# Swapping a unit's similarities with a gather, and loading the first image by channel chunk

## The reference

```python
xn  = x / max(norm(x, axis=1), EPS)              # x: (8, 512, 32, 48), float32
cn  = centroids / max(norm(centroids, axis=1), EPS)       # 40 centroids of 512
sim = einsum('bchw,nc->bnhw', xn, cn)
idx = argmax(sim, axis=1);  onehot = one_hot(idx, 40)
sum_x = einsum('bhwn,bchw->bnc', onehot, x)      # sums of each image's clusters
mean  = sum_x / max(count, 1)
delta = mean[idx] - x                            # the gathered mean, less x
alpha = exp(-mean_over_channels(delta * delta))
y   = x + alpha * delta
out = relu(einsum('oc,bchw->bohw', W, y) + b)    # W: 512 x 512
```

## Time and profile before

| | |
|---|---|
| median of 3 runs | 421.4 us (420.66 to 421.58) |
| the profiled execution | 421.0 us |
| its span | 419.2 us |
| TensorE, matmuls | 410.0 us, 98% of the span |
| VectorE | 335.4 us, 80% |
| ScalarE | 256.0 us, 61% |
| GpSimd | 257.6 us, 61% |
| moved by DMA | 73.94 MB |

### The profile page before, as it was taken

One profiled execution on the slowest core, in us unless ns is written; L12 is line 12 of the kernel. 1 busy time (PEld: TensorE's weight loads), 2 busy tenths in 40 slices (PEclk: granted clock), 3 DMA queues, 4 the chain that ended last, 5 costly groups with the idle time before them and its releaser, 6 DMA issues.

```text
span 419.2 us, 5853 instructions
## 1 busy us (share of the span) xinstructions
PE 410.0 (98%) x2127; PEld 292.1 (70%) x2150; DVE 335.4 (80%) x411; ACT 256.0 (61%) x351; POOL 257.6 (61%) x113
## 2 busy tenths in 40 slices
PE   7999999999999999999999999999999999999996
PEld 6744466775767767775868757777777758777885
DVE  2469979689789889899798898898798997788730
ACT  5665374665764765665855666746756658566641
POOL 2000654993599766993879936996769938334420
PEclk9999999999999999999999999999999999999999
DMA  8999295987389384966669573893857220222223
GB/s 275 309 277 159 55 255 155 297 243 179 123 212 291 102 211 147 275 172 179 223 154 253 195 198 104 237 265 121 220 136 228 100 102 1 102 100 100 96 77 128
DMA packets 70927, 73.94 MB, mean 176 GB/s; under 512 B 2724, under 2 KB 45732, under 8 KB 70900
## 3 DMA queue, kind: packets, MB, share of 16 engines
q1 hardware_dynamic: 70900, 73.58, 63.2%
HBM read 48.40 MB, written 25.17 MB: 175 GB/s over the span
## 4 chain that ended last, share of the span: by engine, by line
PE 90%; DVE 3%; ACT 3%; issue 1%; DMA 1%; SPq 0%; DVEq 0%; ACTq 0%
PE main L886 20%; PE main L887 19%; PE main L888 19%; PE sump L828 9%; PE fa L779 9%; PE gat L861 5%; DMA x<-x 1%; PE fa L788 1%; PE al L868 1%; PE fa L803 1%; DVE xt L350 1%; PE main L929 1%; PE al L874 1%; PE gat L874 1%; PE main L901 1%
## 5 line engine op out<-in xcount | busy, mean ns | idle before, releaser
L886 PE MATMUL main<-yh,wh 128*128 128x512 f32 x376 | 152.8, 406 | 0.7 <-ACT o L602 0.7
L887 PE MATMUL main<-yl,wh 128*128 128x512 f32 x376 | 146.7, 390 | 0.0
L888 PE MATMUL main<-yh,wl 128*128 128x512 f32 x376 | 146.7, 390 | 0.0
L310 POOL TENSOR_TENSOR z<-z,x 128x1024 f32<-128x1024 f32 x42 | 99.8, 2396 | 68.3 <-DVE z L437 68.3
L317 POOL TENSOR_TENSOR yl<-z,yh 128x1024 fp32r<-128x1024 f32 x44 | 105.6, 2420 | 54.9 <-ACT yh L594 54.9
L602 ACT ACTIVATE o<-main,bcol 128x512 f32<-128x512 f32 x96 | 65.3, 682 | 61.8 <-PE main L888 61.7
L886 PEld LDWEIGHTS main<-yh,wh 128*128 128x128 f32 x376 | 70.6, 188 | 21.9 <-issue 5.0
L888 PEld LDWEIGHTS main<-yh,wl 128*128 128x128 f32 x376 | 70.6, 188 | 15.2
L887 PEld LDWEIGHTS main<-yl,wh 128*128 128x128 f32 x376 | 70.7, 188 | 13.8
L324 POOL TENSOR_TENSOR xr<-xt 128x2048 f32<-128x2048 f32 x11 | 51.5, 4681 | 20.8 <-DVE xt L350 20.8
L413 DVE TENSOR_TENSOR z<-gat,x 128x1024 f32<-128x1024 f32 x46 | 56.1, 1219 | 9.3 <-PE gat L861 9.0
(11 more groups left out here) (118 smaller groups left out, 378.7 us busy)
## 6 DMA issues: line engine op xcount, KB each, us to landing
x<-x SPq DMA_DIRECT2D x24, 1024.0 KB, 5.4
out<-o SPq DMA_DIRECT2D x23, 1024.0 KB, 7.2
xs<-x SPq DMA_DIRECT2D x84, 256.0 KB, 5.6
o<-w SPq DMA_DIRECT2D x1, 1024.0 KB, 12.3
out<-o SPq DMA_DIRECT2D x4, 256.0 KB, 2.1
sq<-centroids SPq DMA_DIRECT2D x2, 80.0 KB
bcol<-bias SPq DMA_DIRECT2D x1, 2.0 KB, 11.9
```

The costliest lines, as they stand in the source:

```text
L310: pool.tensor_tensor(z, z, X[g // PARTS % 2][:, pair(h), span(g)], ALU.add).then_inc(y_pool, 1)
L886: t_.matmul(main[:, o % 2, :], WH[:, k, rows], YH[g % 2][:, k, :], start=(k == 0), stop=False)
L887: t_.matmul(main[:, o % 2, :], WH[:, k, rows], YL[g % 2][:, k, :], start=False, stop=False)
L888: last = t_.matmul(main[:, o % 2, :], WL[:, k, rows], YH[g % 2][:, k, :], start=False, stop=(k == KC - 1))
```

## The change

Three things are edited.

1. In an image's second slot the similarities of the next image's third unit stand ahead of the second gather on TensorE, not behind it. ScalarE's copy of them stands ahead of the second square, and VectorE's first half transpose of unit g + 4 ahead of the second difference. There are six such slots, units 4, 7, 10, 13, 16 and 19.
2. Image 0's x is loaded by unit and channel chunk, in twelve DMAs of 256 KB, each with its own semaphore, and the similarities wait for each chunk just before they use it. The counts of the other x semaphores follow. Two of six warming matmuls go.
3. In the first slot of unit 3 alone, the relu of call 1 stands on ScalarE ahead of the second high half, not behind it.

```diff
@@ -153,6 +153,8 @@
             return gat[:, 0, :] if g == 1 else al[:, :]
 
 
+
+        first_in = [[sem(f"first_in{u}_{k}") for k in range(KC)] for u in range(PARTS)]
         x_in = [[sem(f"x_in{j}_{u}") for u in range(PARTS)] for j in range(2)]
         xs_in = [sem(f"xs_in{j}") for j in range(2)]
         w_in, b_in = sem("w_in"), sem("b_in")
@@ -230,6 +232,10 @@
                 if b >= 2:
                     for h in range(2):
                         wait_y(sp, g - 2 * PARTS, h)
+                if b == 0:
+                    for k in range(KC):
+                        sp.dma_start(X[0][:, k, span(g)], x_rows[0, :, k, span(g)]).then_inc(first_in[u][k], 16)
+                    return
                 sp.dma_start(X[b % 2][:, :, span(g)], x_rows[b, :, :, span(g)]).then_inc(x_in[b % 2][u], 16)
 
             def load_xs(g):
@@ -523,9 +529,11 @@
                     transpose_half(g + 3, 1)
                 scale(g - 1, 0)
                 scale(g - 1, 1)
+                if beside and p == 1:
+                    transpose_half(g + 4, 0)
                 delta(g, 1)
                 y_half(g - 1, 1)
-                if beside and p < 2:
+                if beside and p == 0:
                     transpose_half(g + 4, 0)
                 if beside and p == 2:
                     low_clusters(b + 1)
@@ -723,9 +731,11 @@
                     relu(g - 2, 0)
                     if g == PARTS:
                         exp(g - 1)
+                    if beside and p == 1:
+                        copy_sims(3 * b + 5)
                     square(g, 1)
-                    if beside:
-                        copy_sims(3 * b + 3 + 2 * p)
+                    if beside and p == 0:
+                        copy_sims(3 * b + 3)
                     high_half(g - 1, 0)
                     if beside and p == 0:
                         copy_sims(3 * b + 4)
@@ -734,8 +744,10 @@
                     move_upper(g)
                     if not beside:
                         high_sum(g)
+                    if g == PARTS:
+                        relu(g - 2, 1)
                     high_half(g - 1, 1)
-                    if beside and p == 0:
+                    if beside and p == 0 and g > PARTS:
                         relu(g - 2, 1)
                     if beside:
                         high_sum(g)
@@ -762,7 +774,8 @@
 
             def similarities(g):
                 b, u = divmod(g, PARTS)
-                pe.wait_ge(x_in[b % 2][u], 16 * (b // 2 + 1))
+                if b > 0:
+                    pe.wait_ge(x_in[b % 2][u], 16 * ((b + 1) // 2))
                 if b == 1:
                     pe.wait_ge(ohT_done, 1)
                 wait(pe, g_ready, b if b > 1 else 0)
@@ -770,6 +783,8 @@
                     pe.wait_ge(simS_done, PARTS * b + 1)
                 rows = X[b % 2]
                 for k in range(KC):
+                    if b == 0:
+                        pe.wait_ge(first_in[u][k], 16)
                     for h in range(2):
                         toks = rows[:, k, span(g)]
                         if plain(b):
@@ -913,7 +928,7 @@
             for k in range(KC):
                 last = t_.transpose(sumP[:, k * N:(k + 1) * N], craw[0:N, k * P:(k + 1) * P], ident[0:N, 0:N])
             last.then_inc(cT_ps, 1)
-            keep_busy(6)
+            keep_busy(4)
             pe.wait_ge(cT_done, 2)
             def transpose_weights(k):
                 pe.wait_ge(w_in, 16)
@@ -996,12 +1011,12 @@
                     convolve(g - LAG, 0)
                     if g == PARTS:
                         sum_squares(g - 1)
+                    if beside and p == 1:
+                        similarities(3 * b + 5)
                     gather(g, 1)
                     if beside and p == 0:
                         similarities(3 * b + 3)
                         similarities(3 * b + 4)
-                    if beside and p == 1:
-                        similarities(3 * b + 5)
                 convolve(g - LAG, 1)
                 if beside and p == 1:
                     transpose_sims(b + 1)
```

## The result

The changed kernel takes 429.89 us (median of 4 runs, 429.55 to 430.63), the kernel before 421.42 in the same comparison: a ratio of 1.0212, with a 95% interval of 1.0199 to 1.0224. That is slower by some 8.5 us. The forecast was 428.6, in a range of 425.0 to 431.0.

What follows compares the result with a forecast made beforehand. TensorE, 98% busy, was taken to bound the kernel, so only work or waits given to it or taken from it count. 421.0 + 9.0 (second slots) - 0.84 (unit 3's relu) - 0.6 (chunks) = 428.6 us, range 425.0 to 431.0.

Steps and rivals of the forecast that it cites:

- two rooms of 0.73 and 0.26 us: Second slots: slack before TensorE's fourth convolution waits for ScalarE's relu (0.73), and before the cluster sums wait for VectorE's transpose (0.26).
- The shift of the second difference, 1.72: Second slots, VectorE: the difference after the second gather starts at 136.30 instead of 134.58, 1.72 us later.
- Nothing shrinks along the chain: Second slots, VectorE and ScalarE: no gap from difference to relu, argmax and half transpose can shrink; all move by 1.72 us.
- The second wait decides; 1.5 a slot, 9.0 in all: Cluster sums' wait for the half transpose sets TensorE's delay: 1.5 us a slot, 9.0 for six, from 6.0 to 11.4.
- Unit 3's relu, 0.84: Unit 3's first slot: TensorE's 0.73 us wait and 0.11 of a longer matmul go, gaining 0.84, from 0.7 to 0.9.
- Chunks and fewer warming matmuls, 0.6: Start: first similarities begin at about 5.6 us and end about 8.5 against 9.1, gaining 0.6, from -0.25 to 0.9.
- The limit that I had named: Start: VectorE's half transpose waits for a DMA until 24.55, ahead of the low sums, so at most 0.9 us comes through.
- The rule against the chunks: Image 0's x loads: guidance of at least 1 MiB per DMA; at its 64 KB speed the sum ends some 13 us higher.
- the rival that I priced by the row at 203 GB/s: Start: the x chunks stream slowly, unit 2 lands at about 19.8, total 434.5 us; chance 0.03.
- The delay is not swallowed: Judges the rival that the second-slot chain absorbs the shift between gather and relu, leaving 419.0 us; chance 0.07.
- Only the relu wait counts: Second slots: argmax and transpose close up by 0.5, so each slot costs 1.04, total 425.8 us; chance 0.07.
- gains and costs don't cancel: Judges the rival that gains and costs cancel, at about 0.3 us per slot, total 421 us; chance 0.03.

Runs made afterwards that it cites:

- the run with the relu early: Changed kernel, with the relu of call 1 in second slots ahead of the move of the upper half on ScalarE: 430.2 us, ratio 1.0229.
- the runs with and without chunks: First pair: changed kernel with old second-slot order, 419.9; kernel before with only unit 3's relu moved, 419.83. Second pair: all edits plus relieved waits, 419.31 with chunks, 419.46 without.
- all together without chunks: Changed kernel with second-slot relu, half transpose, two argmax steps early, unit 3's rearranged load first, but 1 MB x loads and six warming matmuls: 419.46 us, ratio 0.9965.

## Why the prediction was right

Point by point, by its own steps.

- *TensorE is full and has nothing to win; room decides.* Right: two rooms of 0.73 and 0.26 us became two waits, in six slots each, and no other wait repeats.
- *The shift of the second difference, 1.72.* Measured 1.76. The step to the similarities, for which I had added 0.04, is 0.08 longer than usual: they start at 134.19, 0.31 behind the last convolution matmul, where a matmul follows another in 0.23.
- *Nothing shrinks along the chain.* Right: relu 1.76, half transpose 1.75. Moving VectorE's first half transpose gains nothing: shown by the run that left it, 430.0.
- *The second wait decides; 1.5 a slot, 9.0 in all.* Right in mechanism: the run with the relu early is as slow as the change. The size is 1.63 a slot and 9.8 in all. Of the 0.13 a slot that were missing, 0.03 is the shift (1.75 at the transpose and not 1.72), 0.05 the handover of 0.14 (146.53 + 1.24 to 147.91) for which I had 0.09, and 0.05 a slip: I subtracted 145.95 where the row says 145.90. The two waits came as 1.05 and 0.34 for 1.1 and 0.5 forecast, since the first costs 1.22 by the slot's end and not 1.0.
- *Unit 3's relu, 0.84.* Between unit 3's similarities and unit 4's gather it is 12.46 us (68.05 to 80.51) against 13.42 (68.35 to 81.77): 0.96. Run alone, it takes the time down by 0.3% (0.2% to 0.4%), with no cost in the next slot.
- *Chunks and fewer warming matmuls, 0.6.* This term was too large. In the changed kernel's trace the means' last step is 0.27 earlier (31.39 against 31.66), on average over the traces 0.1, and the runs with and without chunks can't be told apart (419.9 and 419.83; 419.31 and 419.46). The step that failed is that TensorE would speed up at the same instant, about 7.7 us: in the changed kernel it is slow until past 8.2, and over the traces the instant moves from about 6.6 to past 8.6, so that the first similarities take anything from 2.44 to 3.55 us. The 0.27 of this one trace is a draw from that. The limit that I had named, the half transpose's DMA, stood in the way as well, and later than I had it: 25.31 and not 24.55. The issues were hidden, as I had it: SP issues unit 3's rearranged pieces from 8.90 on, against 8.69. But I had taken the transfers as undisturbed by nine more DMAs, and they are slower.
- *The rule against the chunks.* The Trainium skill, "DMA: Bandwidth & Descriptors", section "Bandwidth", speaks for large DMAs. The trace agrees in sign, 320 against 373 GB/s in the stretch above, and the rival that I priced by the row at 203 GB/s was far too dear. The figures that the prediction quotes from that section of the Trainium skill are of DMAs that GpSimd issues; here SP issues them.
- *The sum.* By the trace 9.8 - 0.96 - 0.27 = 8.6 against the 7.56 forecast; by the spans 427.9 - 419.2 = 8.7. The forecast fell 1.3 us short of the median: 0.8 in the slots and 0.3 at the start, less 0.1 for the relu, and 0.16 by which the median stands above the profiled execution (429.73); the last 0.1 stays open.
- *The rivals.* The delay is not swallowed. "Only the relu wait counts" had it the wrong way round: the relu wait counts only once the transpose is out of the way. And gains and costs don't cancel: it is 10 us against 1.

## What to carry to other kernels

Where one engine is full, moving a step ahead of another on it is priced at what hangs on the step pushed back: follow that to each place where the full engine takes it up again, and compare the shift with the room there. Of several waits at the end of one chain the latest sets the cost; taking an earlier one away gives nothing, and taking the latest away gives only the way to the next. A swap that looks neutral can be made worth something by moving the chain's work into its gaps, and then it is worth what the swap itself saves, here 0.11 us a slot by the trace, too little for the medians to show.

## What the runs showed of the hardware

- TensorE's first similarities take 2.44 to 3.55 us in the nine traces that have the same order and the same warming, while the granted clock reads 1.00, its upper level, in the stretch shown from 4 to 9 us. A matmul with its two loads takes 0.43 us at first and 0.21 later, and the instant of the change moves from about 6.6 to past 8.6 us. Later similarities take 1.95. Of the traces without chunks, with six warming matmuls, that of unit 3's relu alone took 1.95 at once, the kernel before 2.42 and all together without chunks 2.65. So a head start at this place is not a fixed amount.
- Twelve DMAs of 256 KB in place of three of 1 MB, same runs of 2 KB, move 309 to 337 GB/s from 4 to 9 us in nine traces, where the three traces without chunks move 373 to 381, and a load queued behind them landed so that the half transpose started between 24.81 and 25.96 us, in seven traces, against 24.55 and 24.18 in two without chunks.
- In all six second slots of the changed kernel the matmul that follows the wait of 1.05 us hands on 0.1 us later than one in a row: the step behind it starts 0.33 later (143.88 to 144.21 in unit 7's) where 0.23 is usual. It is not the wait alone that does this: in the kernel before the first convolution matmul behind the similarities has no wait, and the next starts 0.34 later (136.14 to 136.48).
